# A separate small stack for head 0, the gate joined to the value product, halved first stacks, and later transposes

## The reference

```
xn = layernorm(x)
q, k, v = 16 heads of width 8 of xn @ w_attn.T + b_attn
att = q @ k.T / sqrt(8), causal
S = relu(att of head 0), column 0 and the diagonal set to 0
FF = cumsum over queries of S, shifted by one query;  att -= FF   (in every head)
keep = the 101 keys of smallest FF in each row (and the diagonal); the rest -inf
y = softmax(att) @ v;  attn = y @ w_proj.T + b_proj
ffn: logits = xn @ gate_w.T + gate_b; two of 8 experts by softmax, gate = count * sum
     sum over experts of gate * (relu(xn @ wi.T + bi + lora_e(xn)) @ wo.T + bo)
out = x + attn + ffn
```

## Time and profile before

| what | value |
|---|---|
| median of 3 runs | 702.92 us (701.24 to 705.35) |
| the profiled execution | 708.08 us, span 706.2 us |
| TensorE busy | 580.2 us, 82% |
| VectorE busy | 497.3 us, 70% |
| ScalarE busy | 372.2 us, 53% |
| GpSimd busy | 431.6 us, 61% |
| granted clock of TensorE, mean | 0.963 |
| first score product of batch 0 | 62.18 us |

### The profile page before, as it was taken

One profiled execution on the slowest core, in us unless ns is written; L12 is line 12 of the kernel. 1 busy time (PEld: TensorE's weight loads), 2 busy tenths in 40 slices (PEclk: granted clock), 3 DMA queues, 4 the chain that ended last, 5 costly groups with the idle time before them and its releaser, 6 DMA issues. The chain is left out here.

```text
span 706.2 us, 16742 instructions
## 1 busy us (share of the span) xinstructions
PE 580.2 (82%) x5527; PEld 394.7 (56%) x5527; DVE 497.3 (70%) x2156; ACT 372.2 (53%) x781; POOL 431.6 (61%) x709
## 2 busy tenths in 40 slices
PE   4834798788988988889788888889888988889995
PEld 1413555565565655666465655666565655656573
DVE  7582865977578765988479775988578755987352
ACT  3552445654565545655465555655565545454552
POOL 6405655585556846587556856587556846467561
PEclk9966899999999999999999999999999999999998
DMA  4052540034000520025000510025000520000000
GB/s 93 8 59 25 63 44 1 17 52 55 2 16 13 64 33 1 16 43 62 5 1 16 82 26 1 17 42 65 2 2 12 63 34 1 1 13 6 1 2 16
DMA packets 27286, 18.99 MB, mean 27 GB/s; under 512 B 5417, under 2 KB 27072, under 8 KB 27200
## 3 DMA queue, kind: packets, MB, share of 16 engines
q1 hardware_dynamic: 27200, 17.91, 18.9%
HBM read 3.22 MB, written 2.10 MB: 8 GB/s over the span
## 5 line engine op out<-in xcount | busy, mean ns | idle before, releaser
L525 POOL TENSOR_SCALAR ar<-ar,mx 128x512 f32<-128x512 f32 (+3 forms) x512 | 283.6, 564 | 226.8 <-DVE mx L1309 226.6
L1309 DVE CUSTOM_DVE_ANT_0 ar<-ps_s,mask 128x512 f32<-128x512 f32 (+3 forms) x512 | 235.5, 482 | 39.7 <-PE ps_s L869 31.1
L882 PE MATMUL ps_t<-ident,ar 128*128 128x128 f32 x1280 | 205.4, 279 | 37.1 <-ACT pr L692 19.9
L692 ACT ACTIVATE pr<-ps_t 128x512 f32<-128x512 f32 (+1 forms) x352 | 189.9, 555 | 67.0 <-PE ps_t L882 63.4
L882 PEld LDWEIGHTS ps_t<-ident,ar 128*128 128x128 f32 x1280 | 155.9, 143 | 82.3 <-POOL ar L525 53.3
L869 PE MATMUL ps_s<-ks,qs 96*128 96x512 bf16 (+3 forms) x512 | 131.3, 309 | 16.1 <-DMA ks<-parts 10.3
L901 PE MATMUL ps_o<-pr,va 128*32 128x128 f32 x2560 | 98.4, 280 | 20.0 <-ACT pr L692 14.9
L677 ACT ACTIVATE h<-ps_m,bi_col 128x512 f32<-128x512 f32 x64 | 44.0, 687 | 99.5 <-PE ps_m L816 99.5
L901 PEld LDWEIGHTS ps_o<-pr,va 128*32 128x32 f32 x2560 | 63.1, 110 | 50.8 <-ACT pr L692 29.3
L869 PEld LDWEIGHTS ps_s<-ks,qs 96*128 96x128 bf16 x512 | 43.2, 100 | 56.1 <-issue 27.8
L816 PE MATMUL ps_m<-zm,b_t 128*128 128x512 f32 x128 | 66.8, 604 | 5.2 <-ACT h L677 5.2
(11 more groups left out here) (222 smaller groups left out, 742.5 us busy)
## 6 DMA issues: line engine op xcount, KB each, us to landing
qs<-parts SPq DMA_DIRECT2D x48, 128.0 KB
ks<-parts SPq DMA_DIRECT2D x48, 128.0 KB
xs<-in_L_attn_x SPq DMA_DIRECT2D x8, 256.0 KB, 2.8
out<-res SPq DMA_DIRECT2D x8, 192.0 KB, 2.1
out<-res SPq DMA_DIRECT2D x8, 64.0 KB, 10.0
ar<-in_L_ffn_wi SPq DMA_DIRECT2D x1, 256.0 KB, 3.2
ar<-in_L_ffn_wo SPq DMA_DIRECT2D x1, 256.0 KB, 3.8
ar<-in_L_ffn_lora_B SPq DMA_DIRECT2D x4, 64.0 KB, 4.2
```

Of the source, the lines that this page charges most:

```text
L525: nc.gpsimd.tensor_scalar(col, col, -1.0, mx[:, t % NA_RING, j:j + 1], ALU.mult, ALU.add)\
L692: nc.scalar.activation(pr[:, u % NP_RING, 0:w], ps_t[u % NT_RING][:, 0:w], ACT.Exp, scale=-1.0)\
L882: last = nc.tensor.transpose(ps_t[u % NT_RING][:, P * j:P * j + P], ar[:, u % NA_RING, P * j:P * j + P], ident[:, :])
L1309: nc.vector.tensor_tensor_reduce(out=ar[:, t % NA_RING, w * j:w * j + w], in0=ps_s[t % NS_RING][:, w * j:w * j + w], in1=mask[:, k % 2, OF ...
```

## The change

1. **Lags.** `LAG_T` 3 becomes 4, `LAG_P` 4 becomes 5.
2. **Small stack.** For batches 2 and on head 0's q and k parts also go to a tile of their own, `first_heads`, by twelve transfers of 8 rows (8 KB). SyncE issues them for batch k + 2 behind the first output part of batch k. Head 0's products read that tile.
3. **Edge by GpSimd.** The second product with `later` goes. GpSimd sets the edge of the relu'd scores to 0 instead (one select of 128 x 128 for each of four tiles), and the scans wait for it.
4. **Gate joined.** `wv` gets the gate's 8 columns; jobs `v` and `gate` become `v0` and `v1`, two blocks of 136 columns each.
5. **First stacks halved.** Stacks of batch 0 go in two rounds, tokens 0 to 255 and then the rest; unit 0 waits for the first round, unit 12 for all. Stacks of batch 1 are issued later on the queue.
6. **Counts of the search** by ScalarE write to `work` in place of a tile of their own.
7. **A new table of steps** for all jobs, batch 0's feed-forward jobs apart (`FIRST_FFN`); the wide tile is selected within the batch before; the bias parts move to the start.

```diff
-LAG_T, LAG_P = 3, 4
-OUT_LAG, OT_LAG, YT_LAG = 0, 2, 4
+LAG_T, LAG_P = 4, 5
+OUT_LAG = 0
...
-HIDDEN_AT = (14, 17, 20, 23)
-FFN_JOBS = [("z", 5, "act"), ("mask0", 7, "dve"), ("mask1", 8, "dve")] + \
-    [(f"h{f}{j}", HIDDEN_AT[f] + j, "act") for f in range(NF) for j in range(2)] + \
-    [("down0", 28, "dve"), ("down1", 30, "dve")]
+FIRST_FFN = ffn_jobs(6, (17, 19), (22, 24, 27, 30), (34, 36))
+FFN_JOBS = ffn_jobs(4, (8, 8), (15, 18, 21, 23), (29, 31))
+OT_AT, YT_AT, PROJ_AT = (12, 19, 36, 50), (17, 22, 39, 52), (40, 55)
...
 FIRST_AT = {
-    "moments": 0, "root": 0, "norm": 1, "xt": 2, "q": 9, "k": 9,
-    "rest_q": 9, "second_q": 10, "third_q": 13, "rest_k": 9, "second_k": 11, "third_k": 13,
-    "gate": 14, "route": 16, "choices": 21, "share": 24,
-    "under": 19, "reach": 20, "marks_narrow": 21, "marks_middle": 21, "marks_wide": 12 + AHEAD,
-    "flag": 24, "mask_0": 24, "mask_1": 24, "mask_2": 24, "v": 25, "last": 15 + AHEAD, "mask_3": 16 + AHEAD,
+    "moments": 0, "root": 0, "norm": 1, "xt": 2, "q": 4, "k": 14, "rest_q": 4, "second_q": 5, "third_q": 6,
+    "rest_k": 14, "second_k": 15, "third_k": 16, "s0": 5, "s1": 6, "s2": 7, "s3": 8, "scan0": 6, "scan1": 7,
+    "marks_narrow": 21, "top0_narrow": 22, "replace0_narrow": 22, "top1_narrow": 22, "replace1_narrow": 22,
+    "flag": 24, "mask_0": 24, "mask_1": 24, "v0": 21, "v1": 26, "marks_middle": 26, "top0_middle": 26,
+    "replace0_middle": 27, "top1_middle": 27, "replace1_middle": 28, "marks_wide": 25, "top0_wide": 25,
+    "replace0_wide": 26, "top1_wide": 26, "replace1_wide": 27, "last": 29, "mask_2": 30, "mask_3": 32,
+    "route": 30, "choices": 37, "share": 38,
 }
 SECOND_AT = {
-    "moments": 3 - AHEAD, "root": 3 - AHEAD, "norm": 21 - AHEAD, "xt": 22 - AHEAD, "q": -1, "k": 0,
-    "gate": 2, "route": 4, "choices": 11, "share": 12,
+    "moments": -23, "root": -23, "norm": -5, "xt": -4, "q": 9, "k": 10, "rest_q": 10, "second_q": 11,
+    "third_q": 12, "rest_k": 11, "second_k": 12, "third_k": 12,
 }
 PREP_AT = {
-    "moments": -18, "root": -17, "norm": -15, "xt": -12, "q": -10, "k": -8,
-    "gate": -1, "route": 1, "choices": 8, "share": 9,
-    "s0": 15, "s1": 16, "s2": 17, "s3": 18, "v": 16, "scan0": 16, "scan1": 17, "scan2": 18, "scan3": 19,
-    "f0": 20, "f1": 21, "f2": 22, "f3": 23,
-    "search": 24,
-    "under": 30, "reach": 31, "marks_narrow": 34, "marks_middle": 34, "marks_wide": 56,
-    "flag": 41, "mask_0": 42, "mask_1": 45, "mask_2": 48, "last": 59, "mask_3": 60,
+    "moments": -22, "root": -17, "norm": -15, "xt": -12, "q": -11, "k": -10, "rest_q": -10, "second_q": -9,
+    "third_q": -8, "rest_k": -9, "second_k": -8, "third_k": -7, "v0": 11, "v1": 13, "route": 14, "choices": 22,
+    "share": 23, "s0": 3, "s1": 5, "s2": 7, "s3": 9, "scan0": 6, "scan1": 6, "scan2": 10, "scan3": 12, "f0": 9,
+    "f1": 12, "f2": 13, "f3": 15, "search": 16, "under": 22, "reach": 23, "marks_narrow": 24,
+    "marks_middle": 26, "marks_wide": 27, "top0_narrow": 24, "top0_middle": 26, "top0_wide": 29,
+    "replace0_narrow": 27, "replace0_middle": 28, "replace0_wide": 30, "top1_narrow": 34, "top1_middle": 31,
+    "top1_wide": 35, "replace1_narrow": 35, "replace1_middle": 31, "replace1_wide": 35, "flag": 37,
+    "mask_0": 38, "mask_1": 38, "mask_2": 41, "mask_3": 45,
 }
-BIAS_AT = 9
+BIAS_AT = -22
...
+                        for lo, hi, done in ((0, 2 * P, halved), (2 * P, T, stacked)) if m == 0 else ((0, T, stacked),):
+                            for t in range(2):
+                                sp.wait_ge(split, 2 * m + t + 1)
+                                stack, part = ((qs, Q_PART), (ks, K_PART))[t]
+                                for j in range(len(part)):
+                                    sp.dma_start(stack[8 * j:8 * j + 8, into(m), :, lo:hi],
+                                                 parts[:, t, part[j], lo:hi]).then_inc(done, 16)
+                    def make_first_heads(m):
+                        wait_full(sp, "s3", m - 1)
+                        for t in range(2):
+                            sp.wait_ge(split, 2 * m + t + 1)
+                            part = (Q_PART, K_PART)[t]
                             for j in range(len(part)):
+                                sp.dma_start(first_heads[8 * j:8 * j + 8, t, :], parts[0:P:NH, t, part[j], :])\
+                                    .then_inc(topped, 16)
...
                     make_stacks(0)
-                    make_stacks(1)
                     fetch(2)
...
+                    make_stacks(1)
...
                         store(sp, k, 0)
+                        if k + 2 < B:
+                            make_first_heads(k + 2)
...
+                            if t == at(f"s{a}", n):
+                                wait_read(pool, f"s{a}", n)
+                                edge = s0[:, FOFF[a]:FOFF[a] + P]
+                                nc.gpsimd.affine_select(out=edge, in_=edge, compare_op=ALU.is_gt, fill=0.0, base=0,
+                                                        pattern=[[1, P]], channel_multiplier=-1).then_inc(ruled, 1)
...
-                                pe.wait_ge(stacked, 192 * (n + 1))
-                                nc.tensor.matmul(m[:, 0:T - P * j], ks[:, c, 0, P * j:P * j + P],
-                                                 qs[:, c, 0, P * j:T], start=True, stop=False)
-                            if n == 0:
-                                pe.wait_ge(const, 2)
-                            last = nc.tensor.matmul(m[:, 0:P], ident16[:, :], later[:, :], start=False, stop=True)
+                                pe.wait_ge(topped, 192 * (n - 1))
+                                last = nc.tensor.matmul(m[:, 0:T - P * j], first_heads[:, 1, P * j:P * j + P],
+                                                        first_heads[:, 0, P * j:T], start=True, stop=True)
...
-                        if o == 0:
+                        if u == 0:
+                            pe.wait_ge(halved, 192)
+                        elif o == 0 or u == LAST[1] + 1:
                             pe.wait_ge(stacked, 192 * (k + 1))
```

More of the change, by code:

```diff
@@ L758, in fill @@
                                                     start=True, stop=True)
-                        elif name == "v":
-                            for a in range(NA):
-                                last = nc.tensor.matmul(m[:, P * a:P * a + P], xnt[:, c, P * a:P * a + P], wv[:, :],
-                                                        start=True, stop=True)
-                        elif name == "gate":
+                        elif name in ("v0", "v1"):
                             wait_read(pe, "xt", n)
```

113 lines of the change are left out of this document (49 added, 64 removed), and 4 rows, old and new, of tables (FIRST_AT, PREP_AT).

## The result

The changed kernel takes 661.14 us (median of 4 runs, 660.16 to 662.39) against 704.13 us for the kernel before on the same chip: a ratio of 0.9402, 95% interval 0.9371 to 0.9434 (the ratios here are those on record, which differ by up to 0.003 from the quotient of the medians). The forecast was 671 us, its range 652 to 693. The profiled execution took 660.72 us with a span of 658.8.

The account below looks back on a forecast made before the run. TensorE was taken to bound each batch, with 12 us of waits. Start and batch 0 -10.7, six batches -20.4, last batch -1.2 sum to -32.3 us: from 702.92 to 671 us, range 652 to 693.

Parts of the forecast that it names:

- (1): Start: halved first stacks move in 13.3 us, land at 42 to 46 us and are no longer last to arrive.
- Rival C: First stacks: pieces set the rate, so halving halves nothing; first scores stay at 62 us, 689 us total; chance 0.03.
- (2): Start: selection of the keys kept is late next; flag product at 46.5 us, first mask begins at 48.9.
- (3): Start and batch 0: first VectorE pass at about 50.3 us, unit 4 at 60.5; together -10.7 us.
- the bound of -17: Start and batch 0: the far bound of the -10.7 us forecast, in us, if VectorE's lead is not needed.
- (4): Steady batch: fewer gate and later-mask products, slightly wider value products; -1.15 us of TensorE a batch, on the path.
- (5): Head 0's products in steady batches: small stack leaves 0.5 us of wait a batch and gains 0.6 us.
- Rival B: Head 0's products: the wait moves to the small stack, some 3 us in six batches; 686 us total; chance 0.06.
- (6): Steady batch: transposes four units behind cut GpSimd waits from 2.1 to 1.0 us; 5.0 us for exponentials unchanged.
- (7): Units 6 to 31: VectorE 41.6 us, TensorE 42.4; VectorE outside only 17.5; each of six batches -3.4 us.
- Rival D: Middle of a batch: VectorE becomes the bound if its 16.0 idle us stay; slower, 719 us; chance 0.05.
- Rival A: Whole kernel: only the start pays, six batches and the last give 1 us each; 685 us; chance 0.27.

Follow-up runs that it names:

- e6: Changed kernel with the gate's eight products issued a second time per batch, read by nothing: 665.54 us, ratio 0.9489 to the kernel before.
- e7: Changed kernel with the edge of head 0's scores cut by a second TensorE product again, no GpSimd select: 661.71 us, ratio 0.9433 to the kernel before.
- e1: Changed kernel with the lags alone set back to 3 and 4: 685.05 us, ratio 0.9772 to the kernel before.
- e3: Changed kernel with the small stack's twelve transfers issued ahead of the first output part's store: 665.77 us, ratio 0.9485 to the kernel before.
- e2: Kernel before with the new lags 4 and 5 and nothing else: 715.35 us, ratio 1.0181 to the kernel before.
- e9: Changed kernel with three needless VectorE maxima a batch in the middle, behind units 17, 21 and 25: 670.77 us, ratio 0.957 to the kernel before.
- e10: Changed kernel with three needless VectorE maxima a batch outside the middle, behind units 0, 37 and 41: 661.56 us, ratio 0.9416 to the kernel before.
- e11: Changed kernel with small stack transfers ahead of the store, head 0's last product and first transposed sums one step later: 656.84 us, ratio 0.9348.
- e12: Changed kernel with all four head 0 products, first two scans and first transposed sums one step later, queue unchanged: 678.69 us, ratio 0.9657.
- e4: Changed kernel with batch 0's first stacks sent whole, not halved: 671.31 us, ratio 0.9535 to the kernel before.
- e8: Changed kernel with the next batch's q and k products and their splits back at about their old steps: 682.15 us, ratio 0.9721.

## Why the prediction was right, and where its terms were wrong

- **(1) Halved stacks: right.** Bytes set the rate, at 65 GB/s in 512 B pieces (forecast with 59). Rival C is out.
- **(2) The selection is late next: right.** Flag product 45.46 (46.5 forecast), mask 47.96 (48.9).
- **(3) The first pass was right, the place of unit 4 was the failed step of the start.** First pass 48.98 (50.3 forecast), but unit 4's score product came at 53.51 and not at 60.5. "VectorE sets the pace there" is true (2.10 us of wait in front of unit 4), but I put all of the selection and the passes of four units, 10.2 us, in front of it. With three banks of scores unit 4's product needs only unit 1's pass, which ends just before it: 0.6 us of marks and 2.0 of maxima and replacements had run between the first pass and it. The other 2.4 us of maxima and replacements and the passes of units 2 and 3 followed until 57.6. So of the 7.0 us some 4 are the place, and 3 the size and the earlier first pass. The rest of batch 0 took 132.11 - 53.51 = 78.6 us after 149.08 - 69.2 = 79.9, -1.3 for a forecast of -2. The 6.3 us that the forecast missed in start and batch 0 lie in units 0 to 3, within the bound of -17.
- **(4) TensorE's removed work: right in direction, too large as a time.** In batch 3 busy time fell by 1.68 us (forecast 1.15); e6 and e7 find 0.77 and 0.23 of it. The rest is not traced: with the same products and clock e1 is busy for 67.08 us in batch 3, 0.85 more than the changed kernel, so busy time moves with the schedule too. As length the gate's products give 0.1 to 0.7 us a batch where I had 0.9, and e7 finds nothing to win for the edge's 0.3.
- **(5) The small stack: wrong.** I had 0.5 us of wait a batch and a gain of 0.6; the wait is 11.0 / 6 = 1.8 us, above the 6.5 us in all of before. The failed step is the price of an issue, 0.4 us from a store and loads; these take 0.66, and the product ran 6.4 us after batch 3's start instead of about 3.3. Rival B had the mechanism, though at 7.97 us for twelve, not 9.93 (from the lengths 4.02 + 5.91; the difference of starts that it is written with gives 9.97), and not its outcome. By e3 the wait is no simple loss either: the product behind it had another reason to be late.
- **(6) The lag: right for GpSimd (0.8 us; forecast 1.0), wrong for the exponentials.** "I take no change" for their 5.0 us is the mis-sized term: they fell by 3.5 us in each of batches 1 to 4, some 18 in six batches. e1 and e2 show that the table did most of it, and not which entry. For the lag itself I weighed the old waits (2.1 us) and not what the new table would do to them (4.9), so its worth, 18.7 us in six batches, is far above the 1.1 a batch I gave it.
- **(7) The middle: right.** VectorE 42.33 and TensorE 42.46 us between units 6 and 31 (forecast 41.6 and 42.4), the stretch took 47.08 where I had 48.5, the rest of the batch 28.48 where I had 27.7. Outside VectorE is relieved to 19.4 us, not to 17.5: its work grew by 2.6 us in batch 3, not by 0.4. e9 and e10 show it: work added to VectorE is on the path at the places tried in the middle and off it at those outside. Rival D asked whether the 16 us of idle VectorE could be filled; 4.75 are left. Rival A had six batches gain 1 us each; they gained 5.1.

Batch 3 by terms: busy -1.68, exponentials -3.5, GpSimd -1.3, small stack -0.3, VectorE's bank read +0.5 (0.7 to 0.8 and 0.4), the maximum +2.1 (forecast 1.5), the rest about -0.3: -4.5 (80.06 to 75.56), where the forecast had -3.4. That the two are so near is partly luck: 3.5 us that it didn't expect stand against 2.1 of the maximum, which its sum by terms leaves out. Over six batches it is -5.1 each, with batches 1 and 6 at -7.5 and -8.1 and batches 3 and 4, where both kernels have the full clock, at -4.5 and -3.0. Part of the difference is clock, which I did not forecast: before, batches 1, 2 and 6 have a granted clock under 1.00 (first row of two for batch 2, then batch 6; batch 1 is in the earlier trace rows).

```profile
231.15:311.69 80.54, 69.29 (x691) 48.47 (x687) 59.75 (x266) 45.18 (x95) 52.66 (x87) 0.98 0.21 28
```

```profile
549.11:628.15 79.04, 68.93 (x675) 47.24 (x671) 57.91 (x253) 40.46 (x84) 46.44 (x80) 0.96 0.19 23
```

With (1 - clock) x length, batches 1, 2 and 6 lose 1.6 + 1.6 + 3.2 = 6.4 us by an estimate; in the changed kernel only batch 5 (0.98, 1.5 us) does.

The last batch lost its GpSimd waits, 2.4 to 0.5 us, where I had -1.2, and still takes 78.04 us: TensorE's busy time in its window rose from 64.81 to 66.65 us, with 732 products recorded in it instead of 698. The 34 more are 6 transposes (178 for 172, L900) and 28 value products (384 for 356, L919), 1.7 us of busy time. They are batch 6's: with the larger lags one unit more of its work runs behind the last batch's first score product. I had left that out. The same shift takes such work out of the window of start and batch 0, so the last batch's is in part the other end of the -17.0.

## What to carry to other kernels

A lag between pipeline stages is not a knob with a price of its own: here one unit more costs 12 us in one schedule and gives 24 in the next, so price it against the waits that the new schedule will have. On two engines that are both busy for 0.9 of a stretch, small work costs most of its length there and nothing elsewhere; move it by stretch, not by engine total. Before a wait is removed or moved, look at what its reader waits for next (e3, e11). And read the clock apart from idle time, batch by batch: e12 idles 0.7 us more a batch than the changed kernel, with 2.9 us of it in one piece, and its batches are 2.7 us longer. Between batches with the full clock the 1.5 to 2.0 us of e9 against e10 stand out; in the sum over the batches of one profile, 5 us can be the clock's alone (e4).

## What was not expected of the hardware

- Issuing a transfer of 8 rows of 1 KB from every sixteenth partition takes SyncE 0.66 us (7.97 for twelve), more than the 0.38 for a store of 192 KB. The big stacks behind the twelve are issued from 5.2 us behind the batch's first score product (287.30 and 282.08), where in the kernel before they were issued from 2.7 us ahead of it (309.03 and 311.69).
- Inside the chip's memory 512 B pieces move as fast as 1 KB pieces (65 and 59 GB/s).
- The granted clock falls to half at single TensorE waits of 2.9 and 3.1 us (e12 at 0.50 over 305.4 to 312.2, e8 at 0.51 over 362.9 to 369.8), but the same waits leave it at full in one batch of each, and it also falls behind shorter ones (e3 at a wait of 1.8 us, the changed kernel over 450.9 to 454.3 behind 0.8 and 0.4). Batch 3 of the changed kernel keeps 1.00 with 75.56 - 66.23 = 9.3 us of idle time in pieces of up to 2.2 us.
